# GpSimd sums its own five rows of base values, PE transposes one row in place of five

## What is computed

```python
x = x + _L0_conv_ref(_gn(x), Wq, Wk, Wv, off_w, off_b, attn_w, attn_b, Wo)     # deformable convolution
x = x + _L1_conv_ref(_gn(x), p1_w, p1_b, p2_w, p2_b, p_w, ..., c2_w, c2_b)     # corner pooling
```

```python
sampled = corner(y0, x0, wy0 * wx0) + corner(y0, x1, wy0 * wx1) + corner(y1, x0, wy1 * wx0) + corner(y1, x1, wy1 * wx1)
head_out = jnp.einsum('nhckxy,nhkxy->nhcxy', sampled, awr)
```

## Time and profile before

| | |
|---|---|
| time, median of 3 runs | 133.24 us (132.61 to 133.92) |
| the profiled execution | 133.01 us |
| its span, first to last instruction | 131.1 us |
| PE busy / PEld busy | 115.4 us (88%) / 96.6 us (74%) |
| DVE busy | 95.6 us (73%) |
| ACT busy | 63.9 us (49%) |
| POOL busy | 43.4 us (33%) |
| mean granted clock of PE | 0.995 of full speed |

### The profile page before, as it was taken

How to read it: one execution, slowest core, us unless ns; L and a number is a source line. 1 busy time by engine, 2 the same in 40 slices (tenths; PEclk the granted TensorE clock), 3 DMA queues, 4 the chain that set the end, 5 groups by cost and what they waited for, 6 DMA issues and landing times.

```text
span 131.1 us, 3065 instructions
## 1 busy us (share of the span) xinstructions
PE 115.4 (88%) x1233; PEld 96.6 (74%) x1233; DVE 95.6 (73%) x208; ACT 63.9 (49%) x130; POOL 43.4 (33%) x64
## 2 busy tenths in 40 slices
PE   3999779977899989999899989987979999896970
PEld 2778569975899879998799869965656766565650
DVE  5639999483899196990999869996562989865710
ACT  3969869959953769008693248110301440313100
POOL 8960000509200891009900199960040020222000
PEclk9999999999999999999999999999999999999998
DMA  2840000067899997500000000000000000000033
GB/s 75 242 82 0 0 0 5 0 168 165 187 232 206 234 197 111 134 5 0 0 0 0 5 0 2 0 0 0 7 0 5 5 5 0 0 5 0 0 85 80
DMA packets 8078, 7.34 MB, mean 56 GB/s; under 512 B 4734, under 2 KB 6944, under 8 KB 8064
## 3 DMA queue, kind: packets, MB, share of 16 engines
q1 hardware_dynamic: 7456, 6.62, 23.0%
q10 hardware_dynamic: 608, 0.52, 1.6%
HBM read 2.22 MB, written 0.52 MB: 21 GB/s over the span
## 4 chain that ended last, share of the span: by engine, by line
PE 56%; DVE 20%; issue 8%; ACT 6%; DMA 4%; SPq 2%; POOLq 1%; POOL 1%; DVEq 0%; ACTq 0%
PE bank L1143 11%; PE bank L1095 8%; PE bank L1118 7%; PE bank L1230 6%; PE bank L1083 6%; DVE prod L846 4%; PE bank L1250 4%; DMA bias_s<-in_off_bias 4%; PE bank L1263 3%; PE bank L1129 3%; PE bank L1056 3%; DVE part L854 3%; DVE part L818 2%; ACT cell_t L591 2%; DVE bn L688 2%
## 5 line engine op out<-in xcount | busy, mean ns | idle before, releaser
L854 DVE TENSOR_TENSOR part<-vd,bank 128x512 f32<-128x512 f32 (+2 forms) x25 | 19.8, 834 | 11.6 <-PE bank L1129 10.4
L846 DVE TENSOR_TENSOR prod<-hat,prod 128x576 f32<-128x576 f32 (+2 forms) x25 | 21.3, 916 | 0.4 <-ACT hat L581 0.4
L1143 PE MATMUL bank<-cst,part 128*128 128x128 f32 x168 | 20.1, 274 | 0.4 <-DVE part L854 0.4
L1143 PEld LDWEIGHTS bank<-cst,part 128*128 128x128 f32 x168 | 18.6, 140 | 1.3 <-DVE part L854 1.0
L1118 PE MATMUL bank<-cst,prod 128*128 128x128 f32 x144 | 17.4, 272 | 0.8 <-ACT vd L523 0.8
L1040 PE MATMUL bank<-ones_r 128*128 128x512 f32 x53 | 15.9, 451 | 2.2 <-POOL w_pair L414 2.1
L1118 PEld LDWEIGHTS bank<-cst,prod 128*128 128x128 f32 x144 | 16.1, 141 | 1.3 <-ACT vd L523 0.9
L1095 PE MATMUL bank<-w_cross,g_cross 128*128 128x432 f32 (+1 forms) x90 | 15.5, 320 | 0.4 <-DVE w_cross L831 0.4
L327 POOL TENSOR_TENSOR prod<-prod 128x640 f32<-128x640 f32 (+1 forms) x5 | 6.4, 1274 | 25.8 <-DVE prod L846 25.8
L422 POOL TENSOR_TENSOR ab<-ab,half_pow 128x2 f32<-128x2 f32 (+1 forms) x7 | 5.2, 746 | 29.2 <-DVE ab L701 29.2
L1095 PEld LDWEIGHTS bank<-w_cross,g_cross 128*128 128x128 f32 x90 | 14.2, 190 | 0.9 <-issue 0.5
(11 more groups left out here) (104 smaller groups left out, 185.8 us busy)
## 6 DMA issues: line engine op xcount, KB each, us to landing
vd<-vd SPq DMA_DIRECT2D x2, 840.0 KB, 9.2
vd<-vd SPq DMA_DIRECT2D x2, 784.0 KB, 14.9
vd<-vd SPq DMA_DIRECT2D x2, 300.0 KB, 4.7
prod<-in_w_off SPq DMA_DIRECT2D x1, 486.0 KB, 5.9
vd<-vd SPq DMA_DIRECT2D x2, 224.0 KB, 4.9
w_s<-in_w SPq DMA_DIRECT2D x4, 72.0 KB, 6.4
wc_s<-in_wc SPq DMA_DIRECT2D x2, 144.0 KB, 4.2
wp_s<-in_wp SPq DMA_DIRECT2D x4, 72.0 KB, 2.4
```

Source lines behind the costliest of these rows:

```text
L846: return nc.vector.tensor_tensor(cells[:, STEP0[i]:STEP0[i] + n], hat[:, c % 2, at + 3:at + 3 + n, 0:ck].rearrange("p d (k s) -> p d k s", ...
L854: return nc.vector.tensor_tensor(to.rearrange("p d (q e) -> p d q e", e=HD), moved_by, weights.unsqueeze(3).to_broadcast([P, n, cx, HD]), ...
L1143: last = nc.tensor.matmul(comb_bank[:, j * P:(j + 1) * P], part[:, n % PARTS, d, j * P:(j + 1) * P], ident, start=(m == 0 and d == 0 and j ...
```

## The change

POOL, after its five multiplies of a chunk, adds the five rows in place: the first two rows with the third and fourth in one instruction, then the second row to the first, then the fifth row to the first. Each addition waits for the instruction before it by a new semaphore, `base_parts`, and `base_ready` is raised by an increment of its own when the last is done. PE's `row_sum` transposes one row of base values in place of five in chunks 1 to 3. Nothing else changes; line numbers of the new code are higher by 1 from L238 on and by 11 from L461 on.

```diff
+        base_parts = sem("base_parts")
...
-                last.then_inc(base_ready, 1)
+                last.then_inc(base_parts, 1)
+                rows = part[:, ND - 1, :, 0:w * C]
+                done = 4 * (c - POOL_BASES[0])
+                pool.wait_ge(base_parts, done + 1)
+                nc.gpsimd.tensor_tensor(rows[:, 0:2], rows[:, 0:2], rows[:, 2:4], ALU.add).then_inc(base_parts, 1)
+                pool.wait_ge(base_parts, done + 2)
+                nc.gpsimd.tensor_tensor(rows[:, 0], rows[:, 0], rows[:, 1], ALU.add).then_inc(base_parts, 1)
+                pool.wait_ge(base_parts, done + 3)
+                nc.gpsimd.tensor_tensor(rows[:, 0], rows[:, 0], rows[:, 4], ALU.add).then_inc(base_parts, 1)
+                pool.wait_ge(base_parts, done + 4)
+                pool.sem_inc(base_ready, 1)
...
-                w, nd = CHUNKS[c][1], sum(STEPS_X[i][1] for i in APPLY[c][m]) or ND
+                w, nd = CHUNKS[c][1], sum(STEPS_X[i][1] for i in APPLY[c][m]) or (1 if c in POOL_BASES else ND)
```

## The result

The changed kernel takes 140.99 us in the median of four runs (140.35 to 141.90), the kernel before, run beside it, 132.93: a ratio of 1.060, with an interval of 1.051 to 1.070. The profiled execution took 140.35 us, its span is 138.5 (before: 131.1).

What follows compares the result with a forecast made beforehand. PE was taken to be the bound, with POOL 0.3 us short of being the chain at chunk 4's `cell`. That `cell` coming 6.9 us late, all serial behind it, gave 133.0+6.9=139.9 us, range 134.3 to 142.3.

Steps and rivals of the forecast that it cites:

- The rival of bare adds: POOL's adds in chunks 1 to 3 cost only their own 3.04 us, engines barely interfering; 134.6 us, chance 0.22.
- the one of POOL shut out: DVE's back-to-back stream keeps POOL's adds out until it ends, chunk 4's `cell` 12.1 us late; 145 us, chance 0.10.
- the hidden one: The adds are hidden and 24 fewer transposes save 2.7 us, giving 130.3 us; chance 0.05.
- the engines take turns: POOL's adds and DVE's L888, L893 and L846 alternate in order of asking; 139.9 us, chance 0.52.
- the rule: Where both operands of DVE's instruction are in SBUF, DVE and POOL each hold the other off for a whole instruction.
- Products 2.28 late: Chunk 1: adds alternating with L888, L893 and L846 make DVE's products and POOL's next sums 2.28 us late.
- addition 2 or 3 collide: Chunk 2: add 2 holds L888 off, add 3 goes behind it; L893 and the products come 3.0 us late.
- POOL's queue was to end last: Chunk 4: adds, memsets, then base sums end at 95.05, so DVE takes `cell` at 95.1, 6.9 us late.
- half a clock stood as an upper bound: Chunk 4: PE may fall to 1.2 GHz, making its path 9.1 us late, 2.2 beyond POOL's.
- The sign that DVE would wait there for POOL's base sums: The changed profile would show DVE's L854 on `cell` in chunk 4 waiting for POOL's base sums.
- the likeliest case: POOL and DVE alternate, 139.9 us, or 138 to 142.2 with the clock; chance 0.52.
- hold nothing off: Chunks 3 and 4: mask and border memsets, 3.45 us on POOL's queue, wait for nothing and delay no other instruction.

Runs made afterwards that it cites:

- e1: Kernel before plus three unused POOL additions after the multiplies of chunks 1 to 3, PE still transposing five rows; 140.10 us against 133.01, ratio 1.050.
- e4: Kernel before with the change made in chunk 3 alone; 137.62 us, ratio 1.038.
- e2: Kernel before plus four POOL memsets of a scratch tile, which write and do not read, after the multiplies of chunks 1 to 3; 138.12 us, ratio 1.035.
- e3: Kernel before with the change made in chunk 1 alone; 135.13 us, ratio 1.015.
- e7: Changed kernel with the mask and border memsets moved behind chunk 4's base sums on POOL; 141.03 us, ratio 1.048.
- e11: The changed kernel as it is, timed again beside the version with added useless matmuls; 140.24 us, ratio 1.0505.
- e12: Changed kernel with 12, 18 and 5 useless matmuls where PE waits, timed beside the unaltered changed kernel; 139.81 us, ratio 1.0514.
- e5: Changed kernel with 12, 18 and 5 useless matmuls where PE waits, not timed beside the changed kernel; 141.01 us, ratio 1.050.
- e9: Control: kernel before with only the mask and border memsets moved behind chunk 4's base sums on POOL; 132.70 us, ratio 0.999.
- e6: Changed kernel with the useless matmuls where PE waits, and the mask and border memsets moved behind chunk 4's base sums; 139.98 us, ratio 1.046.

## Why the prediction was right, and where not

**Sign, size and mechanism: right.** 139.9 was forecast, 140.99 and 140.24 measured. The rival of bare adds (134.6) falls by e1 to e4, the one of POOL shut out (145) by the rows of chunk 1, where POOL gets its turns, the hidden one (130.3) by the time. That the engines take turns, which no row had shown, is what the additions of 2.57, 0.82 and 1.72 us show. One of the rows that the prediction drew the rule from does not bear it: L918, which stood for a whole POOL instruction, is a tensor_scalar with one input. For two inputs its rows had only a loss of 0.14 us by DVE's L888 and one of 0.13 by POOL, each at an overlap of 0.27, so the step to whole instructions was a guess that came true; the changed kernel's rows, e1 and e2 are what show it.

**Chunk 1: right.** Products 2.28 late by the prediction, 2.13 by the trace; PE 1.9 late, 2.0 by the trace.

**Chunk 2: wrong in the first trace, right in the second.** The prediction had addition 2 or 3 collide and PE wait for two products of chunk 3. In the first trace all three are bare (1.29, 0.74, 0.74). The step that failed is that it carried no clock into chunk 1: PE's wait of 2.93 us cost it the full clock (1.00 until 57.0, 0.50 in the window from 58 to 60), as this stretch of PE's time line shows,

```profile
56.90 2.43 PE L1094 MATMUL bank<-w_pair,g_pair 128*128 128x432 f32 x8
59.13 2.68 PE L1106 MATMUL bank<-w_cross,g_cross 128*128 128x432 f32 x12
```

where e3 has 1.46 and 2.02. The wait's length alone could not have told it: in e7 PE stood 3.14 us at the same place and kept the full clock. The fall made PE and DVE 1.6 us later again, and the additions were through before DVE came. In e11 and e12 the clock held in chunk 1, and the collision came, on addition 3 in e12 as forecast, on addition 2 in e11. That the first trace came so near the forecast is in part luck: the collision that did not come and the clock that was not in the sum nearly cancel. POOL begins chunk 3's base sums at 77.53, 2.7 us later than before, where 3.0 were forecast.

**Chunk 3: right.** L899 goes ahead of the fifth multiply, the three additions and the products share the next 5 us; PE went on at 89.09, forecast 89.57 (by the time of the row sum in chunk 1 this run was 0.9 us ahead of the one before).

**Chunk 4: right in the sum, wrong in what decides.** POOL's queue was to end last, at 95.05, with 1 us to spare on PE's path, and half a clock stood as an upper bound 2.2 us beyond it. POOL was ready at 94.68, but the clock did fall, and DVE came from PE's path at 95.60, 0.9 later; in e11 94.33 and 95.26. The sign that DVE would wait there for POOL's base sums did therefore not come in the changed kernel. At full clock, in e5 and e12, it came (1.18 and 1.16 us), and POOL's queue decides as the prediction had it, with 6.7 and 6.8 us, on the count above, for the 6.9 forecast. So the likeliest case should have had the clock's fall at chunk 3's wait of over 4 us in it: all traces of this wait show it (4.34, 4.42 and 4.42 us in the changed kernel, e11 and e7), those with the added matmuls excepted.

**What it did not see.** The additions put chunk 1's late DMA on the chain (14% for 4%), since they stand between it and the base row. Its last multiply began between 50.05 and 52.50 in the traces here. In e9, where PE still transposes five rows, 52.50 costs nothing (132.81 us, as the others); in e5, 52.43 left POOL's `cell` ready at 96.05 where e12, with 50.05, has it at 93.79. This is part of the spread between runs of the changed kernel. Nor is it so that the memsets "hold nothing off": the products beside them keep their bare 2.83 us in the kernel before, but L928 stood for 2.31 us, as the last section shows. It lies off the path here and cost the sum nothing. What remains open is the share of each fall of the clock in a single run's time: one fall more or less behind chunk 4 is worth some 1.4 to 1.9 us (44.3 to 44.8 in place of 42.9 from `cell` to the end in e6, e7 and e11), as much as the versions e5, e6, e7 and e12 differ by; in e1 and e2, where it fell earlier, it was 3.8 and 4.7.

## What to carry over

Before work is moved to an idle engine, look at which of its neighbour's instructions run in that time, and whether both read SBUF: here 3 us of additions on POOL cost DVE some 2 us in each chunk where they met its products, and the eight transposes they saved were worth 0.9. An engine's idle share says little about its slack; POOL, 33% busy, was 0.3 us short of being the chain at one place. And where a change makes PE wait, its clock belongs in the sum of the likeliest case.

## What the runs showed of the hardware that was not expected

Memsets on POOL, which only write, hold off small DVE instructions of one input: L928 took 2.31 us for 0.17 in the changed kernel, L924 2.81 in e2, both until POOL's last memset and through several of them in a row, without a turn in between; with the memsets behind (e6, e7) it took 0.17 again. Off the path here, it delays DVE's next steps in e2.

The same wait does not always cost the clock, and its length alone does not tell. Before the base row of chunk 1 PE's weight loads stood 2.93 us in the changed kernel's first trace, and the clock fell some 0.4 us after they had gone on (1.00 from 56.5 to 57.0, 0.61 in the mean of 57.0 to 57.5); they stood 2.37 us in e11 and even 3.14 us in e7, and went on at full clock. Before the base row of chunk 3 they stood 3.12 us in e4 and went on at half clock. The weight loads of e7 and of e4:

```profile
57.49 0.20 PEld L1153 LDWEIGHTS bank<-cst,part 128*128 128x128 f32 x2 [3.14 <-POOLq L461]
57.66 1.31 PEld L1093 LDWEIGHTS bank<-w_pair,g_pair 128*128 128x128 f32 x8
...
85.49 0.29 PEld L1158 LDWEIGHTS bank<-cst,part 128*128 128x128 f32 x2 [3.12 <-POOLq L465]
85.77 0.98 PEld L1055 LDWEIGHTS bank<-ones_r 128*128 128x128 f32 x3
```

The eight loads of e7 take 1.31 us where the first trace has 2.19, the three of e4 0.98 where the kernel before has 0.53. Once fallen, the clock was back in the window from 60 to 62 after chunk 1's wait and in that from 94 to 96 after chunk 3's, but stayed at 0.50 from 90 to 106 in e2 and from 96 to 108 in e1, though in e2 PE was busy for the whole of every window from 96 to 106. What decides between these cases the traces do not show.
